# Two edge aggregations on one core: gathers that wait for the matrix product itself, index copies by the block, and a scan for the maximum in three wide passes

## The reference

```python
# layer 1: attention over the edges (softmax by target), then a weighted sum of the sources' rows
h = x @ Wn.T + bn
a = leaky_relu(sum((h[src] + edge_attr @ We.T + be) * attn), 0.01)
a = exp(a - segment_max(a, dst)[dst])
out = segment_sum(h[src] * (a / segment_sum(a, dst)[dst])[:, None], dst)
# layer 2: top-2 of 8 experts
# layer 3: a weighted sum of the sources' rows, then batch norm and relu
h = x @ W
agg = segment_sum(edge_weight[:, None] * h[src], dst) + bias
# layer 4: a graph-attention gate, then top-2 of 4 experts
```

## Time and profile before

| | |
|---|---|
| Median of three runs | 3885.39 us |
| Profiled execution | 3854.0 us |
| Its span | 3851.9 us |
| `a0` gathers, first start to last start | 705.2 to 1505.8 us, 462 of them |
| `a1` gathers, first start to last start | 2453.1 to 3103.5 us, 444 of them |
| Busy over the span: PE, DVE, ACT, POOL | 69%, 39%, 20%, 49% |

### The profile page before, as it was taken

How to read it: one execution, slowest core, us unless ns; L and a number is a source line. 1 busy time by engine, 2 the same in 40 slices (tenths; PEclk the granted TensorE clock), 3 DMA queues, 4 the chain that set the end, 5 groups by cost and what they waited for, 6 DMA issues and landing times. The chain is left out here.

```text
span 3851.9 us, 46754 instructions
## 1 busy us (share of the span) xinstructions
PE 2660.5 (69%) x10550; PEld 1816.4 (47%) x10551; DVE 1510.2 (39%) x3666; ACT 759.3 (20%) x2605; POOL 1889.8 (49%) x1926
## 2 busy tenths in 40 slices
PE   3249688465566556699999997677777755989900
PEld 2225587233333333576767665333333334666600
DVE  5774555656666653322222223322222233000075
ACT  0136000123322222222222221111111112222200
POOL 0000666265656554366666663366666611666602
PEclk9555555566666665799999998666666665999955
DMA  2012344132222222100000000233333311110001
GB/s 73 27 38 66 143 146 147 33 83 75 79 79 79 74 76 61 33 11 12 12 12 12 14 1 20 77 91 91 91 89 92 89 26 34 20 20 8 9 36 36
DMA packets 124782, 213.24 MB, mean 55 GB/s; under 512 B 56098, under 2 KB 82807, under 8 KB 122423
## 3 DMA queue, kind: packets, MB, share of 16 engines
q0 software_dynamic: 75808, 125.28, 13.1%
q1 hardware_dynamic: 48918, 87.37, 6.7%
HBM read 196.99 MB, written 15.52 MB: 55 GB/s over the span
## 5 line engine op out<-in xcount | busy, mean ns | idle before, releaser
L589 POOL DMA_INDIRECT a0rows<-table,a0idx x462 | 466.3, 1009 | 363.0 <-ACT a0idx L574 250.5
L589 POOL DMA_INDIRECT a1rows<-table,a1idx x444 | 420.1, 946 | 315.3 <-ACT a1idx L574 176.6
L619 PE MATMUL a1ps<-a1rows,a1w 128*128 128x256 f32 x888 | 435.5, 616 | 173.2 <-DMA a1rows<-table,a1idx 115.9
L619 PE MATMUL a0ps<-a0rows,a0w 128*128 128x257 f32 x924 | 428.3, 602 | 153.6 <-ACT a0w L789 71.4
L1053 POOL DMA_INDIRECT erecords<-k_rece x416 | 404.5, 972 | 213.3 <-issue 103.2
L881 PE MATMUL f0up<-k_xnT,f0w 128*128 x1280 | 386.0, 457 | 59.4 <-ACT f0hid L913 33.7
L1053 POOL DMA_INDIRECT records<-k_recg x288 | 301.0, 1045 | 226.1 <-POOLq L959 74.2
L1373 POOL DMA_INDIRECT gt_land<-table_gat,gt_source x281 | 265.9, 946 | 287.7 <-DVEq L1402 141.7
L619 PEld LDWEIGHTS a1ps<-a1rows,a1w 128*128 128x128 f32 x888 | 215.5, 284 | 393.2 <-issue 278.2
L619 PEld LDWEIGHTS a0ps<-a0rows,a0w 128*128 128x128 f32 x924 | 233.5, 286 | 345.8 <-issue 176.6
L891 PE MATMUL f0dn<-f0w,f0hid 128*128 128x256 f32 x1600 | 357.6, 380 | 9.2 <-issue 8.6
(11 more groups left out here) (387 smaller groups left out, 3133.3 us busy)
## 6 DMA issues: line engine op xcount, KB each, us to landing
es_ea<-in_eaT SPq DMA_DIRECT2D x16, 1664.0 KB
es_lane<-lane_row SPq DMA_DIRECT2D x16, 832.0 KB
so_rowl<-glane_row SPq DMA_DIRECT2D x32, 256.0 KB
a0rows<-table,a0idx POOLq DMA_INDIRECT x462
a1rows<-table,a1idx POOLq DMA_INDIRECT x444
erecords<-k_rece POOLq DMA_INDIRECT x416
table<-k_tbl SPq DMA_DIRECT2D x10, 650.0 KB, 3.6
records<-k_recg POOLq DMA_INDIRECT x288
```

The costliest lines, as they stand in the source:

```text
L589: pool.indirect_dma_start(rows[:, i, 0:TW], None, table, bass.IndirectOffsetOnAxis(ap=idx[:, i:i + 1], axis=0)).then_inc(gathered[i], 16)
L619: nc.tensor.matmul(sum_of(t), w[:, i, :], rows[:, i, 0:width], start=False, stop=False).then_inc(agg_done, 1)
```

## The change

Four things are changed, all in `emit_aggregate`.

1. `put_indices` copies the indices of a whole block in one instruction, into one half of an `idx` that is twice as long. The wait before it is for the products of the block before the last.
2. POOL waits once for each block for the indices, and before each gather for PE's product that frees the slot, on `agg_done` itself, which now starts at 7 (the waits of ACT and DVE on it are shifted by one). Its loop runs over pairs of blocks. When the number of blocks is odd it issues the gathers of one block more, with indices that no one uses, and at the end it waits until all gathers have landed. ACT adds one to `indexed` at its end to let this block pass.
3. `scan` makes the six masks with one instruction over the block, adds the scores with a second and takes the running maximum with a third. `top` has six slots in place of three, so the clearing (line 691) and the reduction (line 704) are over 768 elements in place of 384.
4. `others`, the wide comparison, is shared by `scan` and `mask_blocks`; for the latter nothing changes.

```diff
-        idx = sb("idx", [P, BG], I32)
+        idx = sb("idx", [P, 2 * BG], I32)
...
-        top = sb("top", [P, BG // 2, P], F32)
+        top = sb("top", [P, BG, P], F32)
...
         def put_indices(act, g, c):
-            for i in range(BG):
-                act.wait_ge(agg_done, g * BG + i + 1)
-                nc.scalar.copy(idx[:, i:i + 1], source[:, bass.ds(c + i, 1)]).then_inc(indexed, 1)
+            act.wait_ge(agg_done, g * BG + 1)
+            nc.scalar.copy(idx[:, bass.ds(g % 2 * BG, BG)], source[:, bass.ds(c, BG)]).then_inc(indexed, 1)
...
-            with pool.Fori(0, total) as g:
+            pairs = pool.snap((pool.snap(total) + 1) // 2)
+            pool.reg_mov(count, 1)
+            pool.reg_mov(block_count, 0)
+
+            def gather_block(half):
+                pool.reg_add(block_count, block_count, 1)
+                pool.wait_ge(indexed, 1)
+                pool.wait_ge(indexed, block_count)
                 for i in range(BG):
                     pool.reg_add(count, count, 1)
-                    pool.wait_ge(indexed, 1)
-                    pool.wait_ge(indexed, count)
+                    pool.wait_ge(agg_done, 1)
+                    pool.wait_ge(agg_done, count)
                     pool.indirect_dma_start(rows[:, i, 0:TW], None, table,
-                                            bass.IndirectOffsetOnAxis(ap=idx[:, i:i + 1], axis=0)).then_inc(gathered[i], 16)
+                                            bass.IndirectOffsetOnAxis(ap=idx[:, half * BG + i:half * BG + i + 1], axis=0)
+                                            ).then_inc(gathered[i], 16)
+
+            with pool.Fori(0, pairs):
+                for half in range(2):
+                    gather_block(half)
+            landed = pool.snap(pairs * 32)
+            for i in range(BG):
+                pool.wait_ge(gathered[i], 16)
+                pool.wait_ge(gathered[i], landed)
...
-            pe.sem_inc(agg_done, BG)
+            pe.sem_inc(agg_done, BG + 1)
...
-            def mask(to, t, c, i):
-                nc.vector.tensor_scalar(to[:, i, :], S.iota[:, bass.ds(t * P, P)], S.dstf[:, bass.ds(c + i, 1)], -BIG,
-                                        ALU.not_equal, ALU.mult)
+            def others(to, t, c):
+                nc.vector.tensor_tensor(to[:], S.iota[:, bass.ds(t * P, P)].unsqueeze(1).to_broadcast([P, BG, P]),
+                                        S.dstf[:, bass.ds(c, BG)].unsqueeze(2).to_broadcast([P, BG, P]), ALU.not_equal)
...
-                    for i in range(BG):
-                        mask(mb, t, c, i)
+                    others(mb, t, c)
                     v.drain()
-                    for i in range(BG):
-                        if i == BG // 2:
-                            v.drain()
-                        nc.vector.scalar_tensor_tensor(top[:, i % (BG // 2), :], mb[:, i, :], S.score[:, bass.ds(c + i, 1)],
-                                                       top[:, i % (BG // 2), :], ALU.add, ALU.max)
+                    nc.vector.scalar_tensor_tensor(mb[:], mb[:], -BIG, S.score[:, bass.ds(c, BG)].unsqueeze(2).to_broadcast([P, BG, P]),
+                                                   ALU.mult, ALU.add)
+                    v.drain()
+                    nc.vector.tensor_tensor(top[:], top[:], mb[:], ALU.max)
                     v.drain()
```

More of the change, by code:

```diff
@@ L581, in _ @@
                 total = pool.value_load(S.eranges[0:1, NT:NT + 1], min_val=1, max_val=EBLOCKS)
-            count = pool.alloc_register(tag + "_count")
-            pool.reg_mov(count, 0)
-            with pool.Fori(0, total) as g:
+            pairs = pool.snap((pool.snap(total) + 1) // 2)
+            count, block_count = pool.alloc_register(tag + "_count"), pool.alloc_register(tag + "_blocks")
+            pool.reg_mov(count, 1)
[4 more added lines that the diff above has]
+                pool.wait_ge(indexed, block_count)
                 for i in range(BG):
                     pool.reg_add(count, count, 1)
-                    pool.wait_ge(indexed, 1)
-                    pool.wait_ge(indexed, count)
+                    pool.wait_ge(agg_done, 1)
+                    pool.wait_ge(agg_done, count)
                     pool.indirect_dma_start(rows[:, i, 0:TW], None, table,
-                                            bass.IndirectOffsetOnAxis(ap=idx[:, i:i + 1], axis=0)).then_inc(gathered[i], 16)
+                                            bass.IndirectOffsetOnAxis(ap=idx[:, half * BG + i:half * BG + i + 1], axis=0)
[7 more added lines that the diff above has]
+                pool.wait_ge(gathered[i], landed)
         @block.tensor
         def _(pe):
-            pe.sem_inc(agg_done, BG)
+            pe.sem_inc(agg_done, BG + 1)
             tiles = Tiles(pe, "pe")
@@ L656, in _ @@
                         for i in range(BG):
-                            v.wait_ge(agg_done, g * BG + i + 1)
+                            v.wait_ge(agg_done, g * BG + i + 2)
                             nc.vector.tensor_scalar(w[:, i, :], S.iota[:, 0:P], S.elane[:, bass.ds(c + i, 1)],
@@ L668, in _ @@
                     put_indices(act, g, slot_of(nc, act, g, EBLOCKS, BG))
+                act.drain().then_inc(indexed, 1)
             return
@@ L721, in mask_blocks @@
                     c = tiles.chunk(g)
-                    nc.vector.tensor_tensor(ne[:], S.iota[:, bass.ds(t * P, P)].unsqueeze(1).to_broadcast([P, BG, P]),
-                                            S.dstf[:, bass.ds(c, BG)].unsqueeze(2).to_broadcast([P, BG, P]), ALU.not_equal)
+                    others(ne, t, c)
                     v.drain()
@@ L787, in _ @@
                     for i in range(BG):
-                        act.wait_ge(agg_done, g * BG + i + 1)
+                        act.wait_ge(agg_done, g * BG + i + 2)
                         nc.scalar.activation(w[:, i, :], nb[:, bass.ds(g % RING, 1), i, :].rearrange("p a n -> p (a n)"), ACT.Exp, bias=S.score[:, bass.ds(c + i, 1)]).then_inc(weighed, 1)
+            act.drain().then_inc(indexed, 1)
 def wait_for_event(pool, event, up_done, down_done):
```

## The result

The changed kernel takes 3846.58 us (median of four runs, 3840.99 to 3848.32), beside 3887.89 us for the kernel before (four runs, 3881.91 to 3893.16). The ratio is 0.9892, 95% interval 0.9873 to 0.991: faster by 41 us, where 101 us were forecast. The profiled execution of the changed kernel took 3847.32 us, its span is 3845.5 us. That is only 6.4 us under the span before, because the one execution profiled before (3854.0 us) was an uncommonly quick one. A second profile of the same kernel, taken for this, has a span of 3896.2 us, and a third one 3888.0 us.

The account below looks back on a forecast made before the run. DVE was taken to bound the first aggregation and POOL's gathers the second. Terms of -39 and -62 us sum to -101, taking the profiled 3854.0 to 3753; plus 31 for timed runs, 3785 us, range 3715 to 3865.

Parts of the forecast that it names:

- the first kind: Second aggregation: 46 POOL stalls where ACT's index copy is late though the product is long done; removing them gives -72 us.
- rival 1: PE's count is late for every engine, so the second aggregation gains only 25 us: 3821 us in all; chance 0.16.
- Late weights: Second aggregation: with earlier gathers, DVE's weights become the next thing late; +15 us, bounds 0 and 34.
- The second kind: Second aggregation: 13 POOL stalls where the product itself is late at PE's tile change; 0.4 us saved on each, -5 us.
- The scan block: First aggregation, DVE: a new scan block takes 3.80 us instead of 3.95, over 77 blocks -12 us.
- The reduction: First aggregation, DVE: 768 elements instead of 384 take 0.96 to 1.0 us instead of 0.592, +10 us.
- The sequencer's losses: First aggregation: DVE's sequencer loses 100 us in the scan; fewer instructions save half of it, -50 us.
- Rival 2: The sequencer's loss is a fixed time per tile and stays; first aggregation +11 us, 3834 us in all; chance 0.10.
- POOL in the first aggregation: POOL's gathers, slowed 44 us by new wide passes, need 742 us, under DVE's 771, so DVE stays the bound.
- Rival 3: The wide scan starves POOL, most first-aggregation gathers taking 1.46 us: +90 us there, 3913 us in all; chance 0.10.
- The sum of the first aggregation: First aggregation: -43 us on DVE's chain plus 4 us for landing the extra gathers, -39 us; bounds -92 and +90.
- Rival 4: All stalls go: -80 us in the first aggregation, -90 in the second, 3715 us in all; chance 0.16.

Follow-up runs that it names:

- e12: Only the new gathers and index copies, old scan, exponentials held until the block before's products are done, against the kernel before on a 3509.80 us chip: 0.9983.
- e14: Only the new gathers and index copies, old scan, no added wait, against the kernel before on a 3509.80 us chip: 0.9982.
- e0: The kernel before, unedited, profiled a second time: 3898.35 us.
- e9: The kernel before, unedited, with a profile of its own on a slower chip: 3889.78 us.
- e2: Only the new scan, old gathers and index copies, against the kernel before on a 3909.62 us chip: 0.9862.
- e11: Only the new scan, old gathers and index copies, against the kernel before on a 3889.78 us chip: 3834.50 us, 0.9861.
- e8: The whole change again, no new edit, against the kernel before on a 3889.78 us chip: 3858.19 us, 0.9919.
- e1: Only the new gathers and index copies, old scan, against the kernel before on a 3909.62 us chip: 1.025.
- e10: Only the new gathers and index copies, old scan, against the kernel before on a 3889.78 us chip: 1.0266.
- e13: The whole change plus ACT's wait for the block before's products ahead of the exponentials, against the kernel before on a 3509.80 us chip: 0.9974.
- e3: The change with twelve row slots for six in the second aggregation and two more POOL waits a gather, against the kernel before at 3909.62 us: 0.9871.
- e4: The change with bf16 products in the second aggregation, against the kernel before on a 3509.92 us chip: 0.986.
- e7: The whole change plus ACT's wait for the block before's products ahead of the exponentials, against the kernel before on a 3509.92 us chip: 0.9965.
- e17: New scan, old gathers in the first aggregation, new ones in the second, against the kernel before on a 3510.38 us chip: 3493.84 us, 0.9956.

## Why the prediction was wrong, step by step

**The step that failed** is the first term of the second aggregation: "the first kind goes if POOL sees PE's count when it changes", -72 us. It doesn't go. POOL does see the count when it changes, but the count changes late: POOL waits for it directly and is held as long (77.5 us in 51 stalls, after 71.6 in 46), and 41 of the 51 end 0.77 us after a recorded count. With the gathers of this change, the stalls are nearly absent on the 3510 us chips (3.5 to 4.2 us in 4 stalls in e12 to e14). So they come with the chip or the time, and not with the chain of copies. The profile of before had hinted at it: ACT and DVE started within 0.05 us of each other, 5 us after the product. That is rival 1, which I gave 0.16. Why the count is late stays open. With that term at 0 the same working gives 3885 - 39 - 62 + 72 = 3856 us, and with the second aggregation at no change 3846, against 3846.58 measured. That the last agrees so closely is luck: it rests on -39 for the first aggregation, whose terms are off both ways (below).

**Late weights**, +15: the right way and somewhat small. PE's wait for DVE's weights went from 34.4 to 54.0 us; in the other profiles on slower chips it is 38.5 to 43.9 with the old gathers (e0, e9, e2, e11) and 64.3 to 83.4 with the new ones (e8, e1, e10). How much of it lengthens the stage is not shown.

**The second kind**, -5: the hand-over is 0.40 us shorter, as forecast (from product to gather 1.18 us before, 0.78 after). The total of these stalls didn't fall (24.8 to 24.2 us), since there are 16 for 13, and PE is later by the weights. Rival 1 priced 0.42 us on all 59 stalls, -25 us. The hand-over is shorter in the first kind as well (1.16 us from the count to the gather in the earlier trace rows, 0.77 after), and yet that sum didn't fall either. It ranges from 68.5 to 85.7 us in five traces with the old gathers and from 70.8 to 77.5 in four with the new ones, so a gain of 18 us in it can't be made out.

**"Near 590 us"** for the second aggregation: 657.6 here, 594.8 to 598.4 on the 3510 us chips. The price of the work was right, 444 x 1.25 and some 40 us.

**The scan block**, -12: too small. The block of the earlier trace rows was a short one. Where nothing is held up, on the 3510 us chips, an ordinary block takes 4.05 us with the old scan (e14) and 3.78 with the new one (e13), and all 77 together 303 and 280 us, so -24. **Clearing `top`**, +9: 25 x (0.698 - 0.378) = +8. **The reduction**, +10: it took 1.448 us for 0.592, so +21. I had priced it as a pass over 768 elements. It grew by 2.4 where its elements doubled. The arithmetic alone is then worth -24 + 8 + 21, about nothing, where I had +7.

**The sequencer's losses**, half of 100 us: DVE's idle time fell by 50.6 us, so the size is right, but partly by luck. In the scan they are gone nearly whole: the scan blocks took 413.4 us before and 290.7 after, 123 us less, some 24 of which are the arithmetic. But the time from the reduction to the copy of `negm` grew from 18.2 to 51.5 us (21 of it the reduction), and from there to the first mask from 19.7 to 47.8 us. So some 40 us came back at the change of tile. With the scan alone these two stretches took 33 us and 21 to 29; there the stretch from the finish of a tile's sum to the clearing of `top` lost time instead, 29 us in e11 against e9 and 37 in e2 against e0. Rival 2 had this half right: part of the loss falls on whatever runs then.

**POOL in the first aggregation**, under DVE's chain: some gathers are slowed beside wide passes. Two beside the wide masks of the current tile, which stood in the kernel before too, took 1.39 and 1.37 us:

```profile
1005.16 0.96 DVE L738 SCALAR_TENSOR_TENSOR a0nb<-a0ne,a0negm 128x768 f32 x1 [0.34 <-issue]
1005.55 1.39 POOL L594 DMA_INDIRECT a0rows<-table,a0idx  x1 [2.32 <-PE a0ps L633]
...
1006.83 0.96 DVE L699 TENSOR_TENSOR a0ne<-k_iota,k_dstf 128x768 f32 x1 [0.71 <-issue]
1007.24 1.37 POOL L594 DMA_INDIRECT a0rows<-table,a0idx  x1 [0.30 <-PE a0ps L633]
```

But the mean went only from 1009 to 1027 ns, 8 us over all and not the 44 that I added. The new passes hardly slow a gather. The 67 gathers that run beside the wide maximum alone take 946 ns, at most 952, as those beside no wide pass do (945). The 69 beside the new comparison alone take 951. The slow ones stand where the second pass of a pair follows the comparison: 1290 ns on average for the 78 beside both passes of the current tile's masks, 1035 for the 68 beside the first two passes of the scan. Rival 3 is out: with 1.03 + 0.30 = 1.33 us a gather, POOL was far from 1.47. The Trainium skill (SBUF — State Buffer, Who interferes with whom) has DVE and GpSimd under an exclusive lock on shared SBUF ports; the 1.39 us row agrees with it in kind. The wide maximum has two inputs in SBUF as well, and the 946 ns beside it show no such lock, so my "by that rule all three new passes take it" fails for at least that one.

**The sum of the first aggregation**, -39: measured -36, and -50 in the later pair. But that is luck in part: it is a sum of a scan worth more (e2 and e11 against e0 and e9: -57 and -62) and of gathers that take 12 us back, where I had them as a gain for POOL and 4 us of landing. That the gather half could cost 100 us beside the old scan was in none of my cases.

**Rival 4**, all stalls go: no, on these chips.

## What to carry to other kernels

A late start of two engines within 0.05 us of each other is not a chain between them: look for a cause common to both before taking a link out of the chain, and look at when the count that both wait for was recorded. Giving the waiting engine twice the slack (more slots) tests whether a stall hangs on its releaser, but only if the waiting engine's program stays the same; in e3 it didn't, and its stalls were of another kind. Where an engine's sequencer is held up for each instruction, fewer and wider instructions gained 57 and 62 us in the first aggregation at nearly the same arithmetic. A gain of 1% should be measured on more than one chip, with each half of the change alone: what gave 1% on one kind of chip gave 0.3% on the other, in the nearest kernel that was run there.

## What the runs showed of the hardware

- **Two kinds of chip.** The same kernel takes 3888 to 3910 us on some and 3510 us on others. Stages that no run edits differ as well: the first experts' stage takes 780 to 806 us on the first kind and 693 to 695 us on the second.
- **Held-up spots on the slower ones.** There, entries of sequencers, nearly all of them DVE's and ACT's, take 0.64 to 0.73 us in place of 0.04 to 0.06: 262 and 268 such entries in two traces of the kernel before (the first and e9), 139 and 160 in two of the changed one, none in the traces of e4 to e7 and e12 to e17. In e3 POOL has 244 of them. What causes them no trace shows.
- **The record is thinner there.** Each trace from a slower chip holds 16,100 to 17,200 increments of semaphores, each from a faster one about 40,000, for nearly the same program. So the recording itself may have a part in the spots, or suffer from the same cause. Every execution here comes with its recorded span, so none shows the kernel without any recording.
- **One count, several late readers.** In such a spot the count of PE's products goes up as much as 6.4 us after a product's modelled end (7.2 us to its gather, less the 0.77), several steps at once, and several engines act on it together: ACT and DVE 0.05 us apart, ACT and POOL 0.4 us apart in the stall shown of the changed kernel. On the 3510 us chips each of the 444 counts in `a1` follows its product by 0.01 us.
- **Gathers beside wide passes.** A gather beside the wide maximum alone took 946 ns, one beside none 945, one beside both passes of the current tile's masks 1290 on average.
- **A strided reduction.** 128 x 384 elements into 128 took 0.592 us, 128 x 768 took 1.448 us.
